# Latent attention on one core: value rows issued in groups of two on every second step, and scores alternated with maxima on the steps between

## The chip, the cores and the metric

The kernel runs on one core of one Trainium2 chip. The metric is the device time of one launch in microseconds, the median of repeated runs. A profile of one further execution shows what each engine did: TensorE (PE in the profile) multiplies matrices, VectorE (DVE) and ScalarE (ACT) work elementwise and read what TensorE leaves in PSUM, GpSimd (POOL) works elementwise in SBUF, and SyncE (SP) issues transfers. The engines have queues of their own and meet at semaphores.

## The reference

The program is a chain of four residual blocks over `x` of shape (4, 1024, 128): causal attention with clipped scores, latent attention with a mixture of experts behind it, a second causal attention, and a low-rank feed-forward block. The change touches the latent attention alone. Its 16 heads share one key per position:

```python
q = (x @ Wq).reshape(b, t, H, D).transpose(0, 2, 1, 3)
ckv = x @ Wkva
kv_latent, k_rope = (ckv[:, :, :R], ckv[:, :, R:])
kv = (kv_latent @ Wkvb).reshape(b, t, H, NOPE).transpose(0, 2, 1, 3)
...
q = jnp.concatenate([q_nope, _rope(q_rope)], axis=-1)
k = jnp.concatenate([kv, _rope(k_rope)], axis=-1)
v = jnp.concatenate([kv, jnp.zeros_like(k_rope)], axis=-1)
att = jnp.einsum('bhqd,bhkd->bhqk', q, k) / jnp.sqrt(jnp.float32(D))
mask = jnp.tril(jnp.ones((t, t), dtype=bool))
att = jnp.where(mask, att, jnp.float32(-jnp.inf))
att = jax.nn.softmax(att, axis=-1)
y = jnp.einsum('bhqk,bhkd->bhqd', att, v)
```

In the kernel `Wkvb` is folded into the queries and into the output weights, so a head works with 16 latent and 32 rotary numbers per position (48 rows), and the softmax's maximum of each query enters the scores as a 49th row.

## The kernel before

Each attention stage runs 16 items (4 sequences times 4 quads of heads); the latent one is called with the name `am`, `latent=True` and `clip=False`. An item is cut by the causal mask into 9 steps, `g` = 0 to 8, and `item` on TensorE (in `attention`) issues for each step, in the order of `ROW_ORDER`, five pieces:

- `score_unit` (L937), twice: keys times queries for two heads, fp32, 49 rows. The two heads use the upper and the lower half of the array's rows. A unit fills two PSUM banks; there are two units of them (`NSB`), so a unit waits for ScalarE's exponential of the unit before the last (`s_e`).
- `max_pair` (L968, with the mask products of L962), twice: queries times keys for two heads in bf16, for an item ahead of the current one by `LEAD` = 4 steps, so that step `g` handles row (g + 4) mod 9 of `MAX_ROWS`. Rows 0, 3, 5 and 7 are one product of 512 columns without a mask, rows 1 and 2 one with a mask, rows 4, 6 and 8 two products. A pair writes two of three PSUM banks (`M_BUFS` = 3). Each bank is read by one `tensor_reduce` on VectorE (L1174), and a pair waits (`s_mr`) until the first reduction of the pair before it is done.
- `value_row` (L989), once: values times probabilities for four heads, fp32, the four heads in four groups of the array's columns. Step `g` handles row `g - PLAG` with `PLAG` = 2, in steps 0 and 1 that is rows 7 and 8 of the item before. A row waits for its exponentials, for GpSimd's masks on the diagonal (`s_sel`, L1127), and rows 0 and 3 also for ScalarE's copy of the output bank (`copy_output`, L1045).

ScalarE takes the score units in order (L1065, an exponential of 128x1024 each) and copies the output bank at steps 2 and 5. Probabilities are kept for six rows (`PRING`), and the exponential of row `g` waits until value row `g - 6` is done. VectorE runs the reductions in order; after row 8 of `MAX_ROWS`, at step 4, `gather_maxima` (L1184, L1186, L1193) puts an item's maxima together before the next reduction. SyncE then carries them through memory into the 49th row of the next item's queries. Before the first item, `first` on TensorE runs 13 rows of `max_pair` with a filler product (L447) behind each pair. The last item has no maxima ahead of it, nor have steps 5 to 8 of the one before; the first item has no values in steps 0 and 1.

Of the kernel before, what the change touches and what calls it, by code (L numbers as in the profile page):

```python
# [36 lines left out]
ROWS_P = (KB * (KB + 1) // 2) * P // UNIT  # L37
# [37 lines left out]
def build(nc, ins, consts, out):  # L75
    stack = ExitStack()
    with stack:
# [601 lines left out]
        def attention(name, scale, latent, clip):  # L679
# [10 lines left out]
            PLAG, PRING = (3 if clip else 2), 6  # L690
# [6 lines left out]
            if clip:  # L697
                ROW_ORDER = (("score", 0), ("score", 1), ("value", 0))
            elif latent:
                ROW_ORDER = (("score", 0), ("score", 1), ("max", 0), ("value", 0), ("max", 1))  # L700
            else:
                ROW_ORDER = (("score", 0), ("score", 1), ("max", 0), ("score", 2), ("max", 1), ("score", 3), ("value", 0))
            DIMS = MD
            KROWS = DIMS + (0 if clip else 1 if latent else 3)
            n_loads = 5 if latent else LOADS8
# [14 lines left out]
            def units(i, g, j, cnt=1):  # L720

                row = (ROWS_P * i + g) % PRING
                if row < RING_ROWS:
                    return ring[:, row * QUAD + j:row * QUAD + j + cnt, :]
                at = (row - RING_ROWS) * QUAD + j
                return pr_buf[:, at:at + cnt, :]
# [41 lines left out]
            def slot(i, off=0):  # L768
                return (i + off) % NB

            def uses(b, i, off=0):

                return b + (i + off) // NB + 1
# [12 lines left out]
            def count_of(eng, b, i):  # L786

                if isinstance(b, int):
                    return b * NQ + i
                count = eng.alloc_register()  # L790
                eng.reg_mov(count, b * NQ + i)
                return eng.snap(count, donate=True, min_val=i, max_val=(BATCH - 2) * NQ + i)

            def max_row(g, last):

                off, r = divmod(g + LEAD, ROWS_P)
                if last is not None and last + 1 + off >= ITEMS:
                    return None
                return 1 + off, r

            with nc.Block() as block:
                @block.sync
                def _(sp):
# [19 lines left out]
                    def maxima(b, i, off):  # L823
# [16 lines left out]
                        for pr in range(2):  # L840
                            if latent:
                                row = ml_d[bass.ds(n, 1), :, :].rearrange("n (a r) t -> n a r t", r=2)[:, :, pr, :]
                            else:
                                row = mx_d[bass.ds(n, 1), :, :, :]\
                                    .rearrange("n c (a r) t -> (n c) a r t", r=2)[:, :, pr, :]
                            sp.dma_start(qs[64 * pr + DIMS:64 * pr + KROWS, s, :, :], row).then_inc(s_mrow[s], 16)

# [78 lines left out]
                def _(pe):  # L926
                    def score_unit(n, i, g, e):
                        t = EXPS_R * g + e
                        bank = s_bank0 + WIDE * (t % NSB)
                        s = slot(i)  # L930

                        wait_alone(pe, s_e, EXPS * n + t + 1)
                        for k, q0, nq, off in S_UNITS[g]:
                            for w in range(WIDE):
                                p, pr = divmod(WIDE * e + w, 2)
                                rows = slice(64 * pr, 64 * pr + KROWS)
                                mm = nc.tensor.matmul(ps[:, bank + w, off * P:(off + nq) * P],  # L937
                                                      keys(rows, s, p, k),
                                                      qs[rows, s, p, q0 * P:(q0 + nq) * P],
                                                      start=True, stop=True)  # L940
                        mm.then_inc(s_s, 1)

                    def max_pair(m, b, i, off, g, p):
# [13 lines left out]
                        for q, k0, nk, o_ in segs:  # L957
# [7 lines left out]
                            for pr in range(2):  # L965
                                rows = slice(64 * pr, 64 * pr + DIMS)
                                kk = slice(k0 * P, (k0 + nk) * P)
# [6 lines left out]
                    def value_row(n, i, g):  # L974

                        s = slot(i)
                        if clip:
                            pe.wait_ge(s_clip, EXPS * n + EXPS_R * (g + 1) + BASE)
                        else:
                            pe.wait_ge(s_e, EXPS * n + EXPS_R * (g + 1) + NSB + BASE)  # L980
                        pe.wait_ge(s_sel, DIAGS * n + diags_before[g + 1] + BASE)
                        half = 0 if g < A_ROWS else 1
                        if g in (0, A_ROWS):
                            pe.wait_ge(s_oc, 2 * n + half + 1 + BASE)
                        for r, k, q0, nq, off in V_ROWS[g]:
                            lo = q0 - 4 * half
                            for j in range(QUAD):
                                v = vs[:, s, k, 0:VW] if latent else vs[:, s, k, j * VS:(j + 1) * VS]
                                mm = nc.tensor.matmul(  # L989
                                    ps[VW * j:VW * j + V_ROWS_OUT, o_bank + half % O_BUFS, lo * P:(lo + nq) * P], v,  # L990
                                    units(i, r, j)[:, 0, off * P:(off + nq) * P],
                                    start=(k == 0), stop=(g in (A_ROWS - 1, ROWS_P - 1)), tile_position=(0, VW * j),
                                    skip_group_check=True)
                        mm.then_inc(s_pv, 1)
# [18 lines left out]
                    def item(b, i, last):  # L1013
                        s = slot(i)
                        n = count_of(pe, b, i)
                        if has_max:
                            pe.wait_ge(s_mrow[s], 16 * 2 * uses(b, i) + BASE)
                        pe.wait_ge(s_ld[s], 16 * n_loads * uses(b, i) + BASE)
                        for g in range(ROWS_P):
                            ahead = max_row(g, last) if has_max else None  # L1020
                            for step, which in ROW_ORDER:
                                if step == "score":
                                    score_unit(n, i, g, which)
                                elif step == "max":
                                    if ahead is not None:
                                        max_pair(n, b, i, *ahead, which)
                                elif g >= PLAG:
                                    value_row(n, i, g - PLAG)
                                elif last != 0:
                                    value_row(n - 1, i - 1, g - PLAG + ROWS_P)  # L1030

                    def rest():
                        for g in range(ROWS_P - PLAG, ROWS_P):
                            value_row(ITEMS - 1, ITEMS - 1, g)

                    run_items(pe, item, first, rest)

                @block.scalar
# [1175 lines left out]
        project_heads8("p0", w_sb["wq0"][:, :], w_sb["wk0"][:, :], w_sb["wv0"][:, :], True)  # L2214
        end_phase()
        attention("a0", 8.0 ** -0.5, latent=False, clip=True)
        end_phase()
        prepare("am")
        finish_and_project_latent(w_sb["wout0"][:, :])
        end_phase()  # L2220
        attention("am", 0.125, latent=True, clip=False)
        end_phase()
        finish_latent()
# [4 lines left out]
        project_heads8("p1", w_sb["wq1"][:, :], w_sb["wk1"][:, :], w_sb["wv1"][:, :], False)  # L2228
        end_phase()
        attention("a1", 8.0 ** -0.5, latent=False, clip=False)  # L2230
        end_phase()
        finish_and_ffn()
# [86 lines left out]
```

## Time and profile before

| | before |
|---|---|
| median of 3 runs | 1818.73 us (1810.61 to 1827.36) |
| the profiled execution: time, span | 1816.31 us, 1814.6 us |
| mean granted clock of TensorE | 0.953 |
| busy over the span: TensorE / VectorE / ScalarE / GpSimd | 88% / 71% / 62% / 37% |
| latent attention: first filler of `first` to the last value matmul | 453.8 to 1005 us |
| its items, from the first score | 508.05 to 1005 us |
| fp32 value rows, fp32 scores, L1174 reductions in all stages | 464.4, 550.0 and 706.7 us busy |

The views used below are the table by stretch (the stretch, its length, then busy us and number of instructions of PE, of PE's weight loads, DVE, ACT and POOL, then TensorE's granted clock, the DMA engines' busy share and GB/s), and the timeline, whose rows are instructions merged by kind: the start in us, the time they took, engine, line, operation, the tiles written and read with their shape, how many, and in brackets how long the engine had been idle before them and which engine's work ended that. The duration of a matmul row holds the modelled time until its results are out, so the difference of two starts tells how long TensorE was occupied. A matmul of fp32 stands in the trace twice.

### The profile page before, as it was taken

What the parts mean: (1) busy time and instruction counts of PE and PEld (TensorE: products, weight loads), DVE (VectorE), ACT (ScalarE), POOL (GpSimd) and SP (SyncE); (2) the same over time, 40 slices, a digit from 0 to 9 for tenths busy, and PEclk for the clock granted to TensorE, in tenths of its full rate; (3) what the DMA queues carried; (4) which work ended last, traced back from release to release, by engine and by line L of the source; (5) the groups of instructions that cost most, each with busy time, mean ns of one, the idle gap of its engine ahead of it and who ended that gap; (6) DMA issues with size and microseconds to landing.
All of it is one profiled execution on the core that took longest, in us unless ns stands there. A gap on an engine that the chain in (4) does not pass through costs nothing. (4 is left out here: it accounts for less than half of the span.)

```text
span 1814.6 us, 36604 instructions
## 1 busy us (share of the span) xinstructions
PE 1598.9 (88%) x12310; PEld 696.2 (38%) x12310; DVE 1293.7 (71%) x2458; ACT 1128.7 (62%) x1788; POOL 674.7 (37%) x1223
## 2 busy tenths in 40 slices
PE   5888888597899999999999888897589999999787
PEld 3422222243344444444444554454333333333233
DVE  6688888676667777777772346664499999999064
ACT  6699999443046565555556434322628888888655
POOL 6566766676313232323222001102513333333373
PEclk9799999799979999999999999988899999999998
DMA  8643434257323131413210400000712222222201
GB/s 236 157 69 58 69 68 135 55 134 174 59 36 78 44 83 43 78 48 72 54 43 25 170 28 1 0 0 1 227 31 52 52 52 52 52 52 70 61 14 47
DMA packets 92080, 125.99 MB, mean 69 GB/s; under 512 B 24533, under 2 KB 64085, under 8 KB 91686
## 3 DMA queue, kind: packets, MB, share of 16 engines
q1 hardware_dynamic: 89814, 121.30, 28.9%
q10 hardware_dynamic: 2096, 2.47, 0.4%
q8 instruction: 101, 1.65, 0.4%
q14 instruction: 69, 0.57, 0.1%
HBM read 76.03 MB, written 47.58 MB: 68 GB/s over the span
## 5 line engine op out<-in xcount | busy, mean ns | idle before, releaser
L1174 DVE TENSOR_REDUCE o_sb<-ps 128x1 f32<-128x512 f32 (+3 forms) x864 | 706.7, 863 | 150.5 <-PE ps L968 143.5
L1065 ACT ACTIVATE q_buf<-ps 128x1024 f32<-128x1024 f32 (+1 forms) x768 | 567.8, 833 | 232.0 <-PE ps L937 230.8
L1127 POOL TENSOR_SCALAR_AFFINE_SELECT q_buf<-q_buf 128x256 f32<-128x256 f32 x432 | 212.9, 515 | 380.9 <-ACT q_buf L1065 320.4
L1065 ACT ACTIVATE pr_buf<-ps 128x1024 f32<-128x1024 f32 (+1 forms) x384 | 286.1, 834 | 63.1 <-PE ps L937 63.0
L989 PE MATMUL ps<-q_buf,v_buf 128*9 128x512 f32 (+7 forms) x2880 | 306.1, 515 | 13.5 <-POOL q_buf L1127 11.7
L937 PE MATMUL ps<-q_buf 48*128 48x512 bf16 (+7 forms) x1536 | 269.6, 330 | 21.6 <-ACT q_buf L1065 5.4
L937 PE MATMUL ps<-q_buf,k_buf 49*128 49x512 f32 (+3 forms) x1536 | 280.4, 492 | 0.0
L1127 POOL TENSOR_SCALAR_AFFINE_SELECT pr_buf<-pr_buf 128x256 f32<-128x256 f32 x336 | 166.3, 520 | 268.6 <-ACT pr_buf L1065 227.3
L937 PEld LDWEIGHTS ps<-q_buf 48*128 48x128 bf16 (+1 forms) x1536 | 78.7, 94 | 255.9 <-ACT q_buf L1065 133.4
L989 PE MATMUL ps<-pr_buf,v_buf 128*9 128x512 f32 (+7 forms) x1728 | 158.3, 459 | 17.5 <-POOL pr_buf L1127 17.5
L937 PEld LDWEIGHTS ps<-q_buf,k_buf 49*128 49x128 f32 x1536 | 143.3, 188 | 71.2 <-issue 46.8
L1234 DVE TENSOR_SCALAR q_buf<-q_buf 128x1024 f32<-128x1024 f32 x192 | 146.2, 770 | 25.0 <-ACT q_buf L1065 22.1
L447 PE MATMUL ps<-w_wg,identity 128*128 128x512 f32 (+1 forms) x214 | 101.7, 598 | 31.0 <-PEq L112 31.0
L968 PE MATMUL ps<-q_buf 48*128 48x512 bf16 (+3 forms) x768 | 119.1, 325 | 7.7 <-DVE o_sb L1174 6.0
L968 PE MATMUL ps<-k_buf,q_buf 48*128 48x512 bf16 (+3 forms) x768 | 121.9, 330 | 4.6 <-DVE o_sb L1174 4.6
L962 PE MATMUL ps<-causal_k,causal_q 64*128 64x128 bf16 x1024 | 107.2, 219 | 15.7 <-DVE o_sb L1174 14.9
L989 PEld LDWEIGHTS ps<-q_buf,v_buf 128*9 128x9 f32 (+1 forms) x2880 | 55.7, 95 | 136.7 <-issue 106.8
L962 PEld LDWEIGHTS ps<-causal_k,causal_q 64*128 64x128 bf16 x1024 | 54.6, 94 | 113.5 <-DVE o_sb L1174 97.2
L1234 DVE TENSOR_SCALAR pr_buf<-pr_buf 128x1024 f32<-128x1024 f32 x96 | 75.0, 788 | 11.5 <-ACT pr_buf L1065 9.8
L316 DVE BATCH_NORM_STATS2 q_buf<-ps 128x6 f32<-128x128 f32 x96 | 21.3, 285 | 80.9 <-PE ps L2055 56.7
L364 ACT ACTIVATE q_buf<-ps,q_buf 128x128 f32<-128x128 f32 x96 | 36.1, 459 | 64.6 <-POOL q_buf L348 64.6
L989 PEld LDWEIGHTS ps<-pr_buf,v_buf 128*9 128x9 f32 (+1 forms) x1728 | 37.0, 96 | 100.5 <-issue 62.5
(184 smaller groups left out, 1750.3 us busy)
## 6 DMA issues: line engine op xcount, KB each, us to landing
q_buf<-qm_d SPq DMA_DIRECT2D x32, 384.0 KB, 6.7
qm_d<-pr_buf SPq DMA_DIRECT2D x80, 128.0 KB, 2.4
o_d<-pr_buf SPq DMA_DIRECT2D x16, 512.0 KB, 2.7
q_buf<-o_d SPq DMA_DIRECT2D x8, 1024.0 KB, 5.0
q_d<-q_buf SPq DMA_DIRECT2D x48, 128.0 KB, 2.1
k_d<-q_buf SPq DMA_DIRECT2D x48, 128.0 KB, 1.9
k_buf<-km_d SPq DMA_DIRECT2D x32, 192.0 KB, 6.8
q_buf<-q_d SPq DMA_DIRECT2D x60, 96.0 KB
```

What stands on the lines that cost most here:

```text
L316: i = nc.vector.bn_stats(self.bn[:, c % 2, t, :], src[:, t, :])
L364: i = nc.scalar.activation(dst[:, t, :], src[:, t, :], ACT.Identity, scale=self.rstd[:, r, t:t + 1], bias=self.minus_m[:, r, t:t + 1])
L447: nc.tensor.matmul(ps[:, bank, 0:columns], identity[:, :], w_sb["wg"][:, 0:columns], start=True, stop=True)
L937: mm = nc.tensor.matmul(ps[:, bank + w, off * P:(off + nq) * P], keys(rows, s, p, k), qs[rows, s, p, q0 * P:(q0 + nq) * P], start=True, st ...
L962: nc.tensor.matmul(ps[:, bank[pr], (o_ + nk - 1) * P:(o_ + nk) * P], causal_q[rows, :], causal_k[rows, :], start=True, stop=False, skip_gr ...
L968: mm = nc.tensor.matmul(ps[:, bank[pr], o_ * P:(o_ + nk) * P], (qm if latent else qs)[rows, s, p, q * P:(q + 1) * P], km[rows, s, kk] if l ...
L989: mm = nc.tensor.matmul(ps[VW * j:VW * j + V_ROWS_OUT, o_bank + half % O_BUFS, lo * P:(lo + nq) * P], v, units(i, r, j)[:, 0, off * P:(off ...
L1065: nc.scalar.activation(units(i, g, WIDE * e, WIDE), ps[:, bank:bank + WIDE, :], ACT.Exp, scale=scale).then_inc(s_e, 1)
L1127: nc.gpsimd.affine_select(out=blk, in_=blk, compare_op=ALU.is_ge, fill=0.0, base=0, pattern=[[0, 2], [1, P]], channel_multiplier=-1)\
L1174: nc.vector.tensor_reduce(to, sc, AX_X, ALU.max).then_inc(s_mr, 1)
L1234: nc.vector.tensor_scalar(two, two, float(np.exp(-10.0)), float(np.exp(10.0)), ALU.max, ALU.min).then_inc(s_clip, 1)
```

## The change

In the latent stage `values_at(g)` now says which value rows a step runs: none in steps 0, 3, 5 and 7; rows 7 and 8 of the item before in step 1; row 0 in step 2; rows 1 and 2 in step 4; 3 and 4 in step 6; 5 and 6 in step 8. So rows 1, 3, 5 and 7 come one step later than before and the others where they were. A step without values issues score, maxima, score, maxima (`NO_VALUE_ORDER`), where a step with values keeps the order of before. No instruction is added or taken away, and the other two attention stages keep their order.

```diff
+            VALUES_AT = {2: (0,), 4: (1, 2), 6: (3, 4), 8: (5, 6), 10: (7, 8)}
+            NO_VALUE_ORDER = (("score", 0), ("max", 0), ("score", 1), ("max", 1))
+
+            def values_at(g):
+
+                if not latent:
+                    return [g - PLAG]
+                return [r for at, rows in VALUES_AT.items() for r in (rows if at == g else
+                                                                      [r - ROWS_P for r in rows] if at == g + ROWS_P else ())]
+
...
                             ahead = max_row(g, last) if has_max else None
-                            for step, which in ROW_ORDER:
+                            rows = values_at(g)
+                            for step, which in ROW_ORDER if rows else NO_VALUE_ORDER:
                                 if step == "score":
                                     score_unit(n, i, g, which)
                                 elif step == "max":
                                     if ahead is not None:
                                         max_pair(n, b, i, *ahead, which)
-                                elif g >= PLAG:
-                                    value_row(n, i, g - PLAG)
-                                elif last != 0:
-                                    value_row(n - 1, i - 1, g - PLAG + ROWS_P)
+                                else:
+                                    for r in rows:
+                                        if r >= 0:
+                                            value_row(n, i, r)
+                                        elif last != 0:
+                                            value_row(n - 1, i - 1, r + ROWS_P)
```

How the steps stand on TensorE: the first piece is of an item in steady state, step 3 and the beginning of step 4, before. L937 are scores, L968 maxima with their masks in L962, L989 values.

```order
L937 MATMUL ps<-q_buf,k_buf 128x512 x4
L968 MATMUL ps<-k_buf,q_buf 128x512 x2
L989 MATMUL ps<-pr_buf,v_buf 32x384 x4
L989 MATMUL ps<-pr_buf,v_buf 32x128 x4
L968 MATMUL ps<-k_buf,q_buf 128x512 x2
L937 MATMUL ps<-q_buf,k_buf 128x512 x4
L962 MATMUL ps<-causal_k,causal_q 128x128 x2
L968 MATMUL ps<-k_buf,q_buf 128x384 x2
L962 MATMUL ps<-causal_k,causal_q 128x128 x2
L968 MATMUL ps<-k_buf,q_buf 128x128 x2
L989 MATMUL ps<-pr_buf,v_buf 32x256 x4
```

The same place of the changed program, where scores are L947, maxima L978 with masks in L972, and values L999.

```order
L947 MATMUL ps<-q_buf,k_buf 128x512 x2
L978 MATMUL ps<-k_buf,q_buf 128x512 x2
L947 MATMUL ps<-q_buf,k_buf 128x512 x2
L978 MATMUL ps<-k_buf,q_buf 128x512 x2
L947 MATMUL ps<-q_buf,k_buf 128x512 x4
L972 MATMUL ps<-causal_k,causal_q 128x128 x2
L978 MATMUL ps<-k_buf,q_buf 128x384 x2
L972 MATMUL ps<-causal_k,causal_q 128x128 x2
L978 MATMUL ps<-k_buf,q_buf 128x128 x2
L999 MATMUL ps<-pr_buf,v_buf 32x384 x4
L999 MATMUL ps<-pr_buf,v_buf 32x128 x4
L999 MATMUL ps<-pr_buf,v_buf 32x256 x4
```

Value row 1 has left step 3 for step 4, and in step 3 one score unit instead of a value row stands between the two pairs of maxima.

The second place is step 5 of the same item on TensorE, behind the pair of maxima after which VectorE gathers. Before:

```order
L937 MATMUL ps<-q_buf,k_buf 128x512 x4
L968 MATMUL ps<-k_buf,q_buf 128x512 x2
L989 MATMUL ps<-q_buf,v_buf 32x512 x4
L989 MATMUL ps<-pr_buf,v_buf 32x256 x4
L968 MATMUL ps<-k_buf,q_buf 128x512 x2
```

The changed program, steps 5 and 6:

```order
L947 MATMUL ps<-q_buf,k_buf 128x512 x2
L978 MATMUL ps<-k_buf,q_buf 128x512 x2
L947 MATMUL ps<-q_buf,k_buf 128x512 x2
L978 MATMUL ps<-k_buf,q_buf 128x512 x2
L947 MATMUL ps<-q_buf,k_buf 128x512 x4
L972 MATMUL ps<-causal_k,causal_q 128x128 x2
L978 MATMUL ps<-k_buf,q_buf 128x512 x2
L999 MATMUL ps<-q_buf,v_buf 32x512 x4
L999 MATMUL ps<-pr_buf,v_buf 32x256 x4
L999 MATMUL ps<-q_buf,v_buf 32x512 x4
```

Value row 3 (512 and 256 columns) has moved behind the first maxima of step 6, where row 4 follows it.

## Rows read from the trace of the kernel before

**Rows 1.** Table by stretch: inside the clipped stage, and latent items in steady state.

```profile
60.00:400.00 340.00, 282.28 (x2459) 82.68 (x2460) 278.38 (x439) 289.80 (x341) 223.95 (x320) 0.95 0.41 84
530.60:999.00 468.40, 463.12 (x4045) 212.14 (x4042) 335.28 (x596) 281.45 (x306) 129.83 (x266) 1.00 0.25 56
```

**Rows 2.** Timeline, TensorE, steps 3 to 5 of one item in steady state.

```profile
742.11 0.40 PE L968 MATMUL ps<-k_buf,q_buf 48*128 48x512 bf16 x2
742.44 1.07 PE L989 MATMUL ps<-pr_buf,v_buf 128*32 128x384 f32 x16
743.45 0.39 PE L968 MATMUL ps<-k_buf,q_buf 48*128 48x512 bf16 x2
743.67 1.90 PE L937 MATMUL ps<-q_buf,k_buf 49*128 49x512 f32 x8
745.39 0.24 PE L962 MATMUL ps<-causal_k,causal_q 64*128 64x128 bf16 x2
...
746.85 0.23 PE L962 MATMUL ps<-causal_k,causal_q 64*128 64x128 bf16 x2 [0.38 <-DVE o_sb L1174]
...
747.19 1.95 PE L937 MATMUL ps<-q_buf,k_buf 49*128 49x512 f32 x8
748.96 0.39 PE L968 MATMUL ps<-k_buf,q_buf 48*128 48x512 bf16 x2
749.29 1.06 PE L989 MATMUL ps<-q_buf,v_buf 128*32 128x512 f32 x8
750.17 0.61 PE L989 MATMUL ps<-pr_buf,v_buf 128*32 128x256 f32 x8
750.72 0.39 PE L968 MATMUL ps<-k_buf,q_buf 48*128 48x512 bf16 x2
```

**Rows 3.** Timeline, VectorE, the same place: reductions and the gathering.

```profile
746.01 1.29 DVE L1174 TENSOR_REDUCE o_sb<-ps 128x4 f32<-128x512 f32 x2 [0.77 <-PE ps L968]
...
748.80 0.22 DVE L1184 TENSOR_REDUCE mx_sb<-o_sb 128x16 f32<-128x64 f32 x1
...
749.49 1.26 DVE L1174 TENSOR_REDUCE o_sb<-ps 128x1 f32<-128x512 f32 x2
```

**Rows 4.** Timeline, TensorE before the first item: pairs with short fillers between.

```profile
477.35 0.39 PE L968 MATMUL ps<-k_buf,q_buf 48*128 48x512 bf16 x2 [0.32 <-DVE o_sb L1174]
...
478.69 0.39 PE L968 MATMUL ps<-k_buf,q_buf 48*128 48x512 bf16 x2 [0.32 <-DVE o_sb L1174]
...
492.67 0.23 PE L962 MATMUL ps<-causal_k,causal_q 64*128 64x128 bf16 x2 [0.32 <-DVE o_sb L1174]
...
494.13 0.39 PE L968 MATMUL ps<-k_buf,q_buf 48*128 48x512 bf16 x2 [0.32 <-DVE o_sb L1174]
...
496.12 0.39 PE L968 MATMUL ps<-k_buf,q_buf 48*128 48x512 bf16 x2 [0.97 <-DVE o_sb L1174]
```

**Rows 5.** Timeline, TensorE: first item, second pair of step 0, and scores of step 1.

```profile
513.42 0.29 PE L962 MATMUL ps<-causal_k,causal_q 64*128 64x128 bf16 x2 [0.95 <-DVE o_sb L1174]
...
514.01 3.64 PE L937 MATMUL ps<-q_buf,k_buf 49*128 49x384 f32 x16
517.43 0.60 PE L968 MATMUL ps<-k_buf,q_buf 48*128 48x512 bf16 x2
```

**Rows 6.** Timeline, ScalarE, output copy and exponentials of step 5, same item.

```profile
748.32 0.60 ACT L1045 ACTIVATE pr_buf<-ps 128x512 f32<-128x512 f32 x1 [1.63 <-PE ps L937]
748.81 1.94 ACT L1065 ACTIVATE q_buf<-ps 128x1024 f32<-128x1024 f32 x2
```

**Rows 7.** Timeline, last item without maxima: one step on TensorE.

```profile
967.92 1.99 PE L937 MATMUL ps<-q_buf,k_buf 49*128 49x512 f32 x8
969.84 1.06 PE L989 MATMUL ps<-pr_buf,v_buf 128*32 128x512 f32 x8
970.84 1.99 PE L937 MATMUL ps<-q_buf,k_buf 49*128 49x512 f32 x8
```

**Rows 8.** Timeline, ScalarE, the exponentials of that step.

```profile
969.10 1.94 ACT L1065 ACTIVATE q_buf<-ps 128x1024 f32<-128x1024 f32 x2 [0.93 <-PE ps L937]
```

## Prediction, made before the changed kernel ran

> **What bounds the kernel now.** The change lies in the latent stage, so I read the table by stretch first. Over 468.4 us of its steady state TensorE is busy 463.1 us at the full clock, VectorE 335.3 and ScalarE 281.5 [rows 1]. TensorE's order of work sets this stage, and whatever it loses or saves per item counts in full. The timeline of one item then shows where TensorE is not computing. Two things are to be seen.
>
> First, the switches between kinds of product. From a pair of maxima to the next scores it takes 0.22 us (743.45 to 743.67), but from the same pair to a value row 0.33 us (742.11 to 742.44), so entering values costs 0.11 us [rows 2]. A 512-column value row followed by another takes 0.88 us (749.29 to 750.17). One followed by maxima takes 1.01 (742.44 to 743.45, 384 and 128 columns), so leaving values costs about 0.13 us. A switch there and back is 0.24 to 0.25 us. Two score units take 1.72 us (743.67 to 745.39), 0.86 each.
>
> Second, one wait in each item, 0.38 us before the second pair of step 4 [rows 2]. The value row between the pairs has only 256 columns. The second pair waits until VectorE has done the first reduction of the first pair. VectorE had been idle for 0.77 us before that reduction [rows 3], so this is not a queue on VectorE: it is the round trip of a bank, 745.39 to 746.85, 1.46 us. The stretch before the first item shows the same trip for the other forms, since TensorE has only short fillers there and always waits: 1.34 us for a pair of one 512-column product (477.35 to 478.69), 1.46 us again for two products (492.67 to 494.13), and 1.99 us where the gathering comes between (494.13 to 496.12) [rows 4]. In steady state the pair after the gathering never waits, because 1.72 us of scores come before it and a value row after it.
>
> The Trainium skill (TensorEngine Tiling (Array Packing), Key Properties) says that changing the tiling mode drains TensorE. The trace agrees: scores and maxima share one mode and cost nothing between them, values use another, with the 0.24 us above. That rule speaks for the change, and taken alone it would give the faster rival below.
>
> **What the change saves.** Per item there were nine value rows, each with its own way in and out. Now there are five groups, so four switches go: 4 x 0.25 = 1.0 us. Step 4 now has rows 1 and 2 between its pairs, which covers the 1.46 us: 0.38 us of waiting goes. Together 1.38 us per item.
>
> **What it costs.** In a valueless step the work between one pair and the next is one score unit. From the last pair of the step before to the first pair there are 0.22 + 0.86 = 1.08 us, and the trip takes 1.34, a wait of 0.26. If the pair has two products, it occupies TensorE for 0.34 us (746.85 to 747.19) [rows 2], and against 1.20 us stand 1.46, again 0.26. A pair with one mask lies between these forms, and its wait the same. So every pair of steps 0, 3 and 7 waits about 0.26 us: 6 x 0.26 = 1.56 us. In step 5 the first pair waits 0.26, but the second waits for a reduction behind the gathering: 1.99 against 1.08, 0.91 us. [rows 3] carry the same sum: from the second pair of step 4 at 746.85 to the next item's first reduction at 749.49 are 2.64 us; with 0.66 for that reduction (half of 1.29 or so) and the 0.15 us by which 746.85 follows the end of the reduction begun at 746.01, the second pair could start 3.45 us on, and 1.46 + 1.99 is 3.45. Waits on VectorE are then 1.56 + 0.26 + 0.91 = 2.73 us per item.
>
> ScalarE adds a little. Two exponentials take 1.94 us, a copy another 0.49 (748.32 to 748.81) [rows 6]. A valueless step of 2.6 us with its waits still holds both, but the score unit that follows sits behind exponentials that started up to 1.1 us after their scores, and at step 5 behind the copy. I take 0.2 us per item, from nothing to 0.5 (the copy's whole length).
>
> Balance of a full item: 2.73 + 0.2 - 1.38 = **+1.55 us**, 5% of it. Items 1 to 13 are full: 13 x 1.55 = 20.2 us.
>
> The others: in item 0 step 0 the two pairs already stood without values between them, with a wait of 0.95 us [rows 5]; a score unit now fills it. The rest of that item has its steps 3, 5 and 7 (2.2 us of waits), and saves three switches and 0.38 us. Sum: about +0.2 us. The last item has no maxima, its step of scores and one value row takes 2.92 us (967.92 to 970.84) and hides ScalarE. Without the values the scores of the next step come after 1.73 us. But the first exponential starts 1.18 us after the scores (969.10 against 967.92), lasts 1.02 and is seen 0.15 later, so its banks are free at 2.35 us: 0.62 us of wait in each of four steps, and the copy's 0.49 once, 3.0 us in all [rows 7, 8]. Switches there cost 0.20 in (969.84 less 967.92 is 1.92, less 1.72) and 0.12 out, so merging four saves 1.3 us: about +1.7. Item 14 is half of one kind and half of the other: +1.3.
>
> Value rows that come one step later cost nothing elsewhere. Their exponentials are older, not younger. Rows of six steps are kept, and no value row is more than three steps behind. The output copies at steps 2 and 5 wait for rows 8 and 2, which are still done in steps 1 and 4. The transfers of maxima begin at the same place of an item.
>
> **Sum.** 20.2 + 0.2 + 1.3 + 1.7 = 23.4 us, and TensorE restarts after about eight waits per item instead of one (scores behind the wait of [rows 2] take 1.77 us, 747.19 to 748.96, against 1.72), of which a few us may show. I take +24. Against the profiled execution's own 1816.3 us this is 1840.3; that execution lies 2.4 us under the median of 1818.7, so I say **1841 us**, 1.2% above that median.
>
> **Rivals.**
> *Faster: the round trip is hidden.* If the pairs of valueless steps did not wait, the 1.38 us of each full item would be all: 13 x 1.38 and a little for the others, 20 us less, 1798 us. It decides at a round trip of 1.08 us instead of 1.34. For it: VectorE is idle 28% of the stage [rows 1]. Against it: the trips of [rows 2, 4] were measured with VectorE idle or just keeping up, and three banks let no pair run further ahead. Break-even would be half the waits. Chance 0.08.
>
> *No change that can be measured: half the waits.* The 1.34 us of [rows 4] may be VectorE's pace of two reductions (1.26 to 1.29 us) and not the trip. A pair that finds VectorE idle could then be quicker, and the first pair of each valueless step would not wait: 4 x 0.26 = 1.04 us less per item, +10 us in all, 1829 us. Against it is the 1.46 us from an idle VectorE. Chance 0.20.
>
> *Slower still: ScalarE binds.* If every score unit of a valueless step waited as in the last item, 0.62 x 4 in place of my 0.2, partly inside the waits on VectorE: +1 us per item, 1855 us. Chance 0.07.
>
> *Slower still: the clock.* At the lower level the scores of one step take 3.42 us (514.01 to 517.43) [rows 5] against 1.72. TensorE will now stand idle about 9% of the stage, in pieces under 1 us. In the clipped stage it is busy 83% of 340 us and the granted clock averages 0.95 [rows 1], so I expect the full clock to hold. If as large a share of the stage were lost as there, 5% of 490 us at the lower level adds some 25 us: 1865 us. The Trainium skill (TensorE: Matmul & The Clock Gate, A second HAM failure mode: psum-queue depth-cycling) describes a kernel whose short idle times between groups made the clock swing between its levels. The latent stage's own waits are too few before the change to test that. Chance 0.06.
>
> *The forecast* keeps 0.59, with 1834 to 1849 for its unknown terms: ScalarE's 0 to 0.5 us per item, switches of 0.24 to 0.32, and restarts.
>
> **Chances.** About 1% is what a measurement of this kernel can tell from no change. Slower by more than that means above 1837: most of the forecast (0.50) and both slower rivals (0.13), 0.63. Within 1%: the rest of the forecast, half the waits, and a part of the faster case, 0.31. Faster: 0.06. The range 1826 to 1856 leaves out the faster case, the clock, and little more.
>
> **What would show it.** In the changed profile: maxima of the valueless steps with an idle time of about 0.26 us released by VectorE, and one of 0.9 us an item, eight such waits instead of one; a spacing of 1.34 us between plain pairs; an item 1.5 us longer than before; TensorE waiting 2.9 us an item where it waited 0.4, and about 1 us an item less spent in switches; two value rows of 512 columns in 1.73 to 1.90 us. The forecast is wrong if those pairs start without idle time, if a score unit between two pairs of maxima takes more than 0.86 us, or if the clock in the stage falls below 1.00.

## The result, and the profile after

| | before | changed |
|---|---|---|
| median of 10 runs each | 1819.16 us | 1833.22 us |
| ratio | | 1.0074, interval 1.0048 to 1.0100 |
| the profiled execution: time, span | 1816.31, 1814.6 us | 1838.42, 1836.7 us |
| mean granted clock in it | 0.953 | 0.950 |
| first to last output copy of the latent stage (ScalarE) | 474.7 us | 495.6 us |
| one latent item in steady state | 31.08 us | 32.34 us |

The change makes the kernel slower, by 14 us in this comparison; one run on each side, of 2225.18 and 1858.23 us, was in the slower state and counts in the medians but not in the ratio. In a second comparison, where the changed kernel ran again, the ratio was 1.0107 (1.0069 to 1.0145), which is 19 us. Both intervals are wide for a difference of this size, and the traces say why: the latent stage behaves the same in each, while the time spent at the lower clock elsewhere does not (below). The item's time here and further on is the distance of the same output copy in two consecutive items.

The stage's length can be read from the output copies, 32 in each kernel. The view is the line's own, with minimum, median and maximum duration in ns and the first and last start in us. Before:

```profile
L1045 ACT ACTIVATE pr_buf<-ps x32: 597/597/598, 530.6 to 1005.3; 128x512 f32<-128x512 f32 x32
```

The changed kernel:

```profile
L1058 ACT ACTIVATE pr_buf<-ps x32: 597/597/597, 527.9 to 1023.5; 128x512 f32<-128x512 f32 x32
```

The first copy comes 2.7 us earlier, the last 18.2 us later. Of the 2.7 us, 0.5 lie before the first item, whose first scores start at 507.56 instead of 508.05. A further part is that TensorE's stretch at the lower clock over the first steps was 17.1 us long in this execution instead of 20.5; it is at most half of the difference, 1.7 us (an estimate). So up to 2.2 us of the 2.7 are luck of this execution. The rest the change had saved by then: the wait of 0.95 us in step 0 that [rows 5] showed and the one of step 4 are gone, less the new waits of step 3.

The timeline of TensorE in the changed kernel, steps 3 to 6 of one item, answers to [rows 2]:

```profile
746.39 0.23 PE L972 MATMUL ps<-causal_k,causal_q 64*128 64x128 bf16 x2
...
746.73 1.04 PE L947 MATMUL ps<-q_buf,k_buf 49*128 49x512 f32 x4
747.85 0.39 PE L978 MATMUL ps<-k_buf,q_buf 48*128 48x512 bf16 x2
748.06 1.04 PE L947 MATMUL ps<-q_buf,k_buf 49*128 49x512 f32 x4
749.18 0.39 PE L978 MATMUL ps<-k_buf,q_buf 48*128 48x512 bf16 x2
749.40 2.04 PE L947 MATMUL ps<-q_buf,k_buf 49*128 49x512 f32 x8
751.24 0.25 PE L972 MATMUL ps<-causal_k,causal_q 64*128 64x128 bf16 x2
...
751.71 1.50 PE L999 MATMUL ps<-pr_buf,v_buf 128*32 128x384 f32 x24
753.14 0.23 PE L972 MATMUL ps<-causal_k,causal_q 64*128 64x128 bf16 x2
...
753.49 1.07 PE L947 MATMUL ps<-q_buf,k_buf 49*128 49x512 f32 x4
754.60 0.39 PE L978 MATMUL ps<-k_buf,q_buf 48*128 48x512 bf16 x2
754.82 1.04 PE L947 MATMUL ps<-q_buf,k_buf 49*128 49x512 f32 x4
756.59 0.39 PE L978 MATMUL ps<-k_buf,q_buf 48*128 48x512 bf16 x2 [0.74 <-DVE o_sb L1187]
```

Read the starts of the maxima, not the brackets. From 746.39 to 747.85 are 1.46 us, to 749.18 another 1.33, from 753.14 to 754.60 again 1.46, and to 756.59, over the gathering, 1.99. These are the spacings of [rows 4] within a hundredth. A score unit between two pairs, 0.86 us of work, now takes 1.12 (748.06 to 749.18). Most of these waits have no bracket, because the modelled end of the matmul before covers them: a row of 1.04 us in a slot of 1.12 looks busy. Over the stage TensorE's busy time hides them in the same way.

Step 8 and step 0 of the next item show the same spacing behind a long group of values, for a pair that finds VectorE waiting for work:

```profile
768.25 0.39 PE L978 MATMUL ps<-k_buf,q_buf 48*128 48x512 bf16 x2
768.48 1.02 PE L947 MATMUL ps<-q_buf,k_buf 49*128 49x512 f32 x4
769.59 0.23 PE L972 MATMUL ps<-causal_k,causal_q 64*128 64x128 bf16 x2
```

and on VectorE:

```profile
768.75 1.29 DVE L1187 TENSOR_REDUCE o_sb<-ps 128x1 f32<-128x512 f32 x2 [0.89 <-PE ps L978]
```

VectorE had been idle for 0.89 us, and the next pair still comes 1.34 us after this one.

VectorE at the second place, with the gathering in between, answers to [rows 3]:

```profile
753.76 1.29 DVE L1187 TENSOR_REDUCE o_sb<-ps 128x4 f32<-128x512 f32 x2 [0.59 <-PE ps L978]
755.09 0.22 DVE L1197 TENSOR_REDUCE mx_sb<-o_sb 128x16 f32<-128x64 f32 x1
755.23 0.39 DVE L1199 TENSOR_REDUCE mx_sb<-o_sb 128x4 f32<-128x16 f32 x4
755.65 0.21 DVE L1206 STREAM_TRANSPOSE mx_turned<-mx_sb 128x32 f32<-128x32 f32 x1
755.78 1.26 DVE L1187 TENSOR_REDUCE o_sb<-ps 128x1 f32<-128x512 f32 x2
```

The maxima written at 754.60 are not read before 755.78, and the second pair starts 0.81 us after that.

### The profile page after: what moved, and what is told of

The parts are those of the page before. It is cut to its first block and busy times, and to the rows that moved or that the text cites. A ratio compares the mean times of both kernels' runs of the same rounds, so it can differ in the third digit from the quotient of the medians.

```text
span 1836.7 us, 36604 instructions
## 1 busy us (share of the span) xinstructions
PE 1605.2 (87%) x12310; PEld 696.0 (38%) x12310; DVE 1293.1 (70%) x2458; ACT 1134.6 (62%) x1788; POOL 675.1 (37%) x1223
## 5 line engine op out<-in xcount | busy, mean ns | idle before, releaser
L999 PE MATMUL ps<-q_buf,v_buf 128*9 128x512 f32 (+7 forms) x2880 | 300.7, 514 | 13.6 <-POOL q_buf L1140 11.6
L947 PE MATMUL ps<-q_buf,k_buf 49*128 49x512 f32 (+3 forms) x1536 | 291.4, 492 | 3.1 <-ACT q_buf L1078 1.9
L947 PE MATMUL ps<-q_buf 48*128 48x512 bf16 (+7 forms) x1536 | 270.1, 331 | 20.4 <-ACT q_buf L1078 5.3
L947 PEld LDWEIGHTS ps<-q_buf 48*128 48x128 bf16 (+1 forms) x1536 | 78.8, 94 | 254.8 <-ACT q_buf L1078 132.9
L999 PE MATMUL ps<-pr_buf,v_buf 128*9 128x512 f32 (+7 forms) x1728 | 154.7, 457 | 17.2 <-POOL pr_buf L1140 17.2
L947 PEld LDWEIGHTS ps<-q_buf,k_buf 49*128 49x128 f32 x1536 | 139.9, 188 | 51.7 <-ACT q_buf L1078 17.7
L978 PE MATMUL ps<-k_buf,q_buf 48*128 48x512 bf16 (+3 forms) x768 | 121.5, 330 | 18.2 <-DVE o_sb L1187 15.3
L978 PE MATMUL ps<-q_buf 48*128 48x512 bf16 (+3 forms) x768 | 119.7, 327 | 7.6 <-DVE o_sb L1187 6.0
L447 PE MATMUL ps<-w_wg,identity 128*128 128x512 f32 (+1 forms) x214 | 96.4, 571 | 30.9 <-PEq L112 30.9
L972 PE MATMUL ps<-causal_k,causal_q 64*128 64x128 bf16 x1024 | 107.3, 220 | 14.1 <-DVE o_sb L1187 8.7
L999 PEld LDWEIGHTS ps<-q_buf,v_buf 128*9 128x9 f32 (+1 forms) x2880 | 59.5, 95 | 132.5 <-issue 97.3
L972 PEld LDWEIGHTS ps<-causal_k,causal_q 64*128 64x128 bf16 x1024 | 53.9, 94 | 126.8 <-DVE o_sb L1187 110.4
L1058 ACT ACTIVATE pr_buf<-ps 128x512 f32<-128x512 f32 x64 | 38.1, 595 | 70.7 <-PE ps L947 66.0
L978 PEld LDWEIGHTS ps<-k_buf,q_buf 48*128 48x128 bf16 x768 | 43.3, 95 | 98.5 <-DVE o_sb L1187 68.6
```

What stands on the lines that cost most here:

```text
L447: nc.tensor.matmul(ps[:, bank, 0:columns], identity[:, :], w_sb["wg"][:, 0:columns], start=True, stop=True)
L972: nc.tensor.matmul(ps[:, bank[pr], (o_ + nk - 1) * P:(o_ + nk) * P], causal_q[rows, :], causal_k[rows, :], start=True, stop=False, skip_gr ...
L978: mm = nc.tensor.matmul(ps[:, bank[pr], o_ * P:(o_ + nk) * P], (qm if latent else qs)[rows, s, p, q * P:(q + 1) * P], km[rows, s, kk] if l ...
L999: mm = nc.tensor.matmul(ps[VW * j:VW * j + V_ROWS_OUT, o_bank + half % O_BUFS, lo * P:(lo + nq) * P], v, units(i, r, j)[:, 0, off * P:(off ...
L1058: nc.scalar.activation(o_two[:, i % 2, half * UNIT:(half + 1) * UNIT], ps[:, o_bank + half % O_BUFS, :], ACT.Copy).then_inc(s_oc, 1)
```

## Experiments

**The changed kernel again.** No edit.

> The changed kernel once more, to see how its time moves with the mean granted clock from run to run and whether its item is always 32.34 us long (before: 31.08). Theory: the stage is 18 to 19 us longer in every run, and what differs between runs lies outside it, in stretches at the lower clock; then the ratio is 1.005 to 1.010 and the item in this trace is 32.3 us again. Rival: the stage itself varies; the item would then differ by more than 0.1 us.

Measured: ratio 1.0107 (1.0069 to 1.0145), and 32.33 to 32.35 us for all but a few items, as in the first trace. The stage is the same to 0.1 us (535.4 to 1031.0, 495.5 us). What moves from run to run is the granted clock outside it, and the runs' times follow it, here for the runs of this comparison and of the changed kernel near the same clock:

| mean granted clock of a run | before, us | changed, us |
|---|---|---|
| 0.948 / 0.949 | 1818.26, 1819.78 (0.949) | 1838.44 (0.948) |
| 0.950 / 0.951 | 1818.31, 1818.72, 1816.24 (0.951) | 1840.94 (0.950) |
| 0.954 | 1815.06, 1815.28, 1815.41 | 1835.92 |
| 0.956 / 0.957 | 1810.65, 1814.21, 1812.02 | 1832.06 |
| 0.961 / 0.962 | 1805.33 (0.961) | 1824.39 (0.962) |

A straight line through the compared runs of this study gives, at a mean clock of 0.955, 1813.0 us for the kernel before (70 runs, 1.2 us less for each 0.001 more of clock, scatter 1.5 us) and 1833.0 us for the changed one (14 runs): **20 us** between them. That fits the trace, where the stage ends 18.2 us later after a start that was up to 2.2 us ahead by luck. The mean is taken over the whole launch, and a longer stage at the full clock raises it a little; at equal time spent at the lower clock the same runs lie 19.4 us apart. The medians of the first comparison differ by less: the changed kernel's compared runs there had a mean clock of 0.956, while the median before, 1819.16 us, lies on its line at about 0.950. (The clocks of those runs of before are not known.) Why the mean clock of one batch is higher than that of another I can't say; that stays open.

**Grouped, but without the alternation.**

```diff
-            NO_VALUE_ORDER = (("score", 0), ("max", 0), ("score", 1), ("max", 1))
+            NO_VALUE_ORDER = (("score", 0), ("score", 1), ("max", 0), ("max", 1))
```

> Value rows grouped as in the changed kernel, but valueless steps keep scores, scores, maxima, maxima. Theory (a pair of maxima waits for the bank's trip over VectorE, 1.34 us): in each of four steps the second pair now stands only 0.22 to 0.34 us behind the first and waits about 1.1 us, 4.5 us per item in place of 2.7; item 34.1 to 34.3 us, about 45 us slower than before (ratio 1.022 to 1.026). Rival (the loss of the change comes from score units that wait for ScalarE, and alternation is what delays them): the item is no longer than 32.3 us and the ratio stays under 1.010.

Measured: 1859.87 us, ratio 1.0257 (1.022 to 1.0294), item 33.92 us. TensorE's timeline of this kernel in two valueless steps, step 5 and step 0:

```profile
701.35 0.38 PE L978 MATMUL ps<-k_buf,q_buf 48*128 48x512 bf16 x2
702.68 0.39 PE L978 MATMUL ps<-k_buf,q_buf 48*128 48x512 bf16 x2 [0.95 <-DVE o_sb L1187]
...
716.82 0.22 PE L972 MATMUL ps<-causal_k,causal_q 64*128 64x128 bf16 x2
...
718.27 0.23 PE L972 MATMUL ps<-causal_k,causal_q 64*128 64x128 bf16 x2 [0.95 <-DVE o_sb L1187]
```

The pairs stand next to each other and still start 1.33 us (701.35 to 702.68) and, with two products, 1.45 us apart (716.82 to 718.27). The spacing does not depend on what TensorE does between them. So the alternation is the better half of the change: without it grouping costs 45 us, with it 20. Score units that wait for ScalarE, which the rival named, are not the cause: in steps 5 and 0 here two of them take 1.77 and 1.72 us, as in the kernel before, and the item grew all the same. The item came out 0.2 us under the expected 34.1 to 34.3, which took the second pair of step 5 to wait for the gathering. In this order both score units come before the first pair, and the gathering is over by then.

**Halved reductions, in the changed kernel and in the one before.** The reductions of the latent stage read 256 of 512 columns, so the maxima leave out half of the keys.

```diff
+                            if latent:
+                                sc = sc[:, :, 0:UNIT // 2] if whole else sc[:, :, :, 0:P // 2]
```

> The changed kernel with reductions in the latent stage over half of each bank (256 of 512 columns), so the maxima leave half of the keys out. A reduction should fall from 0.665 us to about 0.40 and the trip from 1.34 to about 1.07 us, just under the 1.08 us of work between two pairs. Theory: the waits of 2.7 us per item fall to about 0.4 (behind the gathering), the item to 30.0 us, 15 to 18 us under the kernel before (ratio 0.990 to 0.993). Rival (ScalarE): nothing on ScalarE changes, the item stays above 31.5 us.

> The kernel before with the same halved reductions, the maxima leaving out half of the keys. Theory: only the one wait of 0.4 us per item is there to fall, item 30.7 us, ratio 0.996 to 0.998. The difference to the halved changed kernel, 0.7 us per item or more, is then what merging four switches is worth without the waits (less the wait behind the gathering). If the halved changed kernel isn't under this one, grouping saves nothing at all.

Measured: item 31.25 us in the changed kernel (31.17 to 31.33) and 30.55 in the one before; ratios 0.9964 (0.9946 to 0.9982) and 0.991 (0.9875 to 0.9945). The kernel before fell by 0.5 us an item, a little more than expected. Besides that its first copy came 14 us earlier (at 516.5 instead of 530.6 us). About half of this is the stretch before the first item, which [rows 4] show waiting for VectorE all the time: from its first pair of maxima to the first scores it took 29.4 us. The kernel with another order in step 4 has whole reductions and in its second trace no lower clock at that place, and took 36.3 (the kernel before 39.1, in part at the lower clock), so the halved reductions are worth about 7 us there. I had not put that into the ratio I expected; it is also why the halved changed kernel is faster than the kernel before although its item is longer. The rest of the 14 us is the clock: the stretch of 20.5 us at the lower clock over the first steps did not come in this execution. The changed kernel missed its 30.0 us by 1.25. Its waits on VectorE went but for about 0.4 us behind the gathering, as expected, and yet only 1.1 us of time came back. TensorE's timeline of that kernel, a valueless step with the first scores of the next:

```profile
715.02 1.02 PE L947 MATMUL ps<-q_buf,k_buf 49*128 49x512 f32 x4
715.89 0.22 PE L972 MATMUL ps<-causal_k,causal_q 64*128 64x128 bf16 x2
...
716.23 1.02 PE L947 MATMUL ps<-q_buf,k_buf 49*128 49x512 f32 x4
717.09 0.22 PE L972 MATMUL ps<-causal_k,causal_q 64*128 64x128 bf16 x2
...
717.43 2.18 PE L947 MATMUL ps<-q_buf,k_buf 49*128 49x384 f32 x16
719.41 0.41 PE L978 MATMUL ps<-k_buf,q_buf 48*128 48x512 bf16 x2
```

The score units in this valueless step take 0.87 and 0.86 us, so no wait on VectorE is left in it. But the two that follow take 1.98 us (717.43 to 719.41) instead of 1.72. The waits view of the same kernel, over twelve items (who waited for whom, us in total, times, longest), says for whom TensorE's weight loads of scores wait:

```profile
PEld ps L947 <- ACT q_buf L1078: 20.8, 54, 0.9
...
PEld ps L947 <- ACT pr_buf L1078: 6.6, 18, 0.6
```

ScalarE needs 1.94 us for two exponentials [rows 8] and its banks come back after 2.35 us, and a valueless step without waits on VectorE is only 2.16 to 2.4 us long. So a second limit stood right behind the first. The rival was right in this much: ScalarE would have taken most of what a quicker VectorE gives back. It was wrong as to the cause of the loss in the changed kernel as it is, where the same loads waited 9.7 us in as long a stretch, and the spacings of 1.33, 1.46 and 1.99 us are VectorE's.

**Halved exponentials as well.** The exponentials of the latent stage cover 256 of 512 columns per head, so half of the probabilities are stale; the reductions stay halved.

```diff
-                                nc.scalar.activation(units(i, g, WIDE * e, WIDE), ps[:, bank:bank + WIDE, :],
+                                cols = UNIT // 2 if latent else UNIT
+                                nc.scalar.activation(units(i, g, WIDE * e, WIDE)[:, :, 0:cols],
+                                                     ps[:, bank:bank + WIDE, 0:cols],
```

> The changed kernel with halved reductions and also exponentials over half of each bank in the latent stage (256 of 512 columns per head), so half of the keys are missing from maxima and half of the probabilities are stale. Theory now: two limits stand one behind the other in a valueless step, VectorE's trip (1.34 us between two pairs) and ScalarE (two score units in 2.35 us), and with both short the saved switches must show: item 30.55 (the halved kernel before) less 1.15 for the switches, plus 0.3 behind the gathering, 29.6 to 29.8 us. Rival: grouping lengthens the item by something else (restarts of TensorE, the gathering); it then stays at 30.5 us or more.

> The kernel before with both halved, the same parts left out. Theory: ScalarE hides nothing there, so the item stays at 30.5 us as with halved reductions alone, and the doubly halved changed kernel is 10 to 14 us faster than this one. Rival: ScalarE also costs the kernel before something; the item falls by more than 0.2 us.

Measured: item 29.73 us grouped and 30.55 us ungrouped, which is 0.8 us less for grouping, in the bounds given. The kernel before did not gain a hundredth from the quicker ScalarE. Over the stage the copies tell the same, first the grouped kernel:

```profile
L1058 ACT ACTIVATE pr_buf<-ps x32: 597/597/597, 514.6 to 971.2; 128x512 f32<-128x512 f32 x32
```

then the ungrouped one:

```profile
L1045 ACT ACTIVATE pr_buf<-ps x32: 597/597/598, 513.3 to 980.1; 128x512 f32<-128x512 f32 x32
```

456.6 against 466.8 us. The measured ratios, 0.9847 (0.9793 to 0.9901) and 0.9861 (0.9825 to 0.9898), overlap, and by them alone the two could not be told apart; at equal mean clock they lie 11 us apart (4 runs each). Grouping does save its switches. It shows only where both readers of PSUM are fast enough to keep up with a step that has no values in it.

**Where in the item the loss lies.** Three kernels differ from the two given only in `VALUES_AT`. The first leaves step 5 alone without values:

```diff
-            VALUES_AT = {2: (0,), 4: (1, 2), 6: (3, 4), 8: (5, 6), 10: (7, 8)}
+            VALUES_AT = {2: (0,), 3: (1,), 4: (2,), 6: (3, 4), 7: (5,), 8: (6,), 9: (7,), 10: (8,)}
```

> The kernel before with only rows 3 and 4 grouped (step 6), so that step 5 alone is valueless and alternated. Theory: 0.26 us before its first pair, 0.9 before the second because of the gathering, 0.28 saved by one switch: item 31.08 + 0.9 = 31.95 us, 12 to 14 us slower than before (ratio about 1.007). Rival (the loss is spread evenly over the four valueless steps): item 31.4 us.

Measured: 1829.82 us, ratio 1.0075 (1.0046 to 1.0105), item 31.91 to 32.06 us. TensorE's timeline around the gathering:

```profile
723.36 0.23 PE L972 MATMUL ps<-causal_k,causal_q 64*128 64x128 bf16 x2 [0.38 <-DVE o_sb L1187]
...
724.82 0.39 PE L978 MATMUL ps<-k_buf,q_buf 48*128 48x512 bf16 x2
...
726.81 0.39 PE L978 MATMUL ps<-k_buf,q_buf 48*128 48x512 bf16 x2 [0.74 <-DVE o_sb L1187]
```

The old wait of step 4 is kept (0.38) and 1.99 us come again between the two pairs (724.82 to 726.81). The second gives step 5 its value row back in the changed kernel:

```diff
-            VALUES_AT = {2: (0,), 4: (1, 2), 6: (3, 4), 8: (5, 6), 10: (7, 8)}
+            VALUES_AT = {2: (0,), 4: (1, 2), 5: (3,), 6: (4,), 8: (5, 6), 10: (7, 8)}
```

> The changed kernel, but value row 3 stays in step 5 and row 4 alone in step 6, so no valueless step follows the gathering. Theory: 0.9 us less than the changed kernel, item 31.4 to 31.5 us, 5 to 6 us slower than before (ratio about 1.003). Rival as for the run with step 5 alone: item 32.0 us.

Measured: item 31.47 to 31.49 us, as expected. The ratio, 0.9995 (0.9964 to 1.0027), does not show the 5 us; at equal mean clock this kernel lies about 5 us above the one before (8 runs). One valueless step of the four, the one behind the gathering, carries 0.87 of the 1.26 us. The rival of an even spread falls.

The third takes the group that looks best, rows 1 and 2, since it also covers the short row's wait:

```diff
-            VALUES_AT = {2: (0,), 4: (1, 2), 6: (3, 4), 8: (5, 6), 10: (7, 8)}
+            VALUES_AT = {2: (0,), 4: (1, 2), 5: (3,), 6: (4,), 7: (5,), 8: (6,), 9: (7,), 10: (8,)}
```

> The kernel before with only rows 1 and 2 grouped (step 4), step 3 alone valueless. It is the one group that also covers a wait of the kernel before (0.42 us behind the 256-column row). Theory: 0.42 + 0.28 saved, 0.51 for two pairs and about 0.12 for ScalarE lost: item 31.0 us, 0 to 2 us faster than before, within what can be measured. Rival (restarts of TensorE cost more than the rows show): item 31.3 us.

Measured: item 31.00 to 31.08 us, ratio 1.0013 (0.998 to 1.0045). No difference. Even the best of the four groups only pays for itself.

**Another order in one step.** In the kernel before, the short value row gets a score unit beside it:

```diff
+            STEP4_ORDER = (("score", 0), ("max", 0), ("score", 1), ("value", 0), ("max", 1))
...
-                            for step, which in ROW_ORDER:
+                            for step, which in STEP4_ORDER if latent and g == 4 else ROW_ORDER:
```

> The kernel before with step 4 alone in another order: score, maxima, score, value, maxima. The short value row then has a score unit beside it between the two pairs, so the wait of 0.42 us goes, and a wait of 0.26 comes before the first pair. Theory: item 30.9 us, 2 to 3 us faster than before in the stage, hardly to be told in the whole time (ratio 0.997 to 1.000). Rival: the order puts the second score unit later and ScalarE with it, item 31.1 us or more.

> The kernel before with step 4 as score, maxima, score, value, maxima, once more in more rounds. The trace of the first run had an item of 30.90 us against 31.08, which is 2.5 us over the stage (ratio 0.9986), while its times came out at 0.996. Theory: the stage's 2.5 us is all there is, and the ratio lies at 0.997 to 1.000. Rival: something outside the stage gains as well, and the ratio stays at 0.996 or below.

Measured: 1809.67 and 1811.85 us, ratios 0.9959 (0.9927 to 0.9992) and 0.9957 (0.9930 to 0.9984), item 30.90 to 30.96 us. TensorE's timeline of step 4:

```profile
710.56 0.39 PE L969 MATMUL ps<-k_buf,q_buf 48*128 48x512 bf16 x2
710.78 1.04 PE L938 MATMUL ps<-q_buf,k_buf 49*128 49x512 f32 x4
711.90 0.23 PE L963 MATMUL ps<-causal_k,causal_q 64*128 64x128 bf16 x2
...
712.24 1.09 PE L938 MATMUL ps<-q_buf,k_buf 49*128 49x512 f32 x4
713.25 0.64 PE L990 MATMUL ps<-q_buf,v_buf 128*32 128x256 f32 x8
713.83 0.23 PE L963 MATMUL ps<-causal_k,causal_q 64*128 64x128 bf16 x2
```

The second pair follows without a wait; the first one is 1.34 us behind the pair before it (710.56 to 711.90), so 0.26 us of the 0.42 are paid there. This kernel is faster than both given ones. The trace accounts for 2.5 us, and at equal mean clock the two batches lie 2.6 and 2.5 us under the kernel before. The other 5 us or so of the measured ratio go with a higher mean clock in its runs (0.956 against 0.951, and 0.954 against 0.950). By the letter of the second expectation the ratio stayed at 0.996, as the rival said. Nothing in the trace of the stage gains more, and what raises the mean clock was not found: chance, or this order itself, which no run separates.

## Why the prediction was right, and where its sizes were off

**The direction and the mechanism** held. The forecast was +24 us and 1841 us; measured were +14 and +19 us in two comparisons, +18.2 us at the end of the stage in the trace, and +20 us at equal clock. 1833.22 us lies inside the range. Of the classes the less likely one came: the result is within 1% of before, to which I gave 0.31, and not above it, to which I gave 0.63. I had set that bound at 1837 us, and both the sum, 4 us too high, and the clock of the runs moved the result across it.

Two of the signs named for a wrong forecast stand in the profile as it is printed. Seven of the eight pairs start without a bracket, and a score unit between two pairs takes 1.12 us, more than 0.86. They were badly worded: the 1.12 us are the work of 0.86 and the forecast wait of 0.26, of which the modelled end of the matmul covers all but 0.08.

**The round trip of a bank**, taken from the stretch before the first item: 1.34, 1.46 and 1.99 us were expected between pairs, and 1.33 to 1.34, 1.46, 1.39 to 1.40 (with one mask) and 1.99 came. Eight waits an item, 2.7 us in sum, as forecast. That a stretch outside the loop had measured the price of an order that did not yet exist was the best evidence in the profile.

**ScalarE in the last item**: 2.35 us to the next scores were worked out. It is 987.33 to 989.68 here, and 2.83 with the copy (1008.37 to 1011.20):

```profile
987.33 1.99 PE L947 MATMUL ps<-q_buf,k_buf 49*128 49x512 f32 x8
989.68 2.05 PE L947 MATMUL ps<-q_buf,k_buf 49*128 49x384 f32 x16 [0.36 <-ACT q_buf L1078]
...
1008.37 1.99 PE L947 MATMUL ps<-q_buf,k_buf 49*128 49x512 f32 x8
1011.20 2.05 PE L947 MATMUL ps<-q_buf,k_buf 49*128 49x512 f32 x8 [0.84 <-ACT q_buf L1078]
```

The forecast gave the last item 1.7 us. The traces have the stretch from step 5 of item 14 to step 5 of the last item, all without maxima, which grew by 1.84 us (28.13 against 26.29 between the copies).

**The terms that were off** are those of the savings, 1.38 us per item. A switch was sized at 0.24 to 0.25 us: 0.11 in and 0.13 out. The 0.13 compared a row followed by another (0.88) with one followed by maxima (1.01), but the first also pays to start. Rows 7 and 8 in the changed kernel's timeline of TensorE (the row names the first of several widths):

```profile
741.12 1.93 PE L999 MATMUL ps<-q_buf,v_buf 128*32 128x512 f32 x24
742.98 0.39 PE L978 MATMUL ps<-k_buf,q_buf 48*128 48x512 bf16 x2
```

Together they take 1.86 us, against twice 1.01 to 1.02 for two such rows apart, so leaving costs 0.16 to 0.18 and a switch 0.27 to 0.29; four of them 1.1 to 1.16 instead of 1.0. The wait of step 4 was taken from the bracket, 0.38. The value row before the change, ahead of the wait of [rows 2]:

```profile
745.84 0.64 PE L989 MATMUL ps<-pr_buf,v_buf 128*32 128x256 f32 x8
```

To the 746.85 of [rows 2] that is 1.01 us. With the other order in step 4 it is 0.58 us (713.25 to 713.83), so the wait was 0.43. Both together are 0.1 to 0.2 us more.

**ScalarE per full item**, 0.2 us, was right for the changed kernel (1.84 us in step 4 and 1.79 in step 8 for 1.72 us of scores). But the kernel before had 0.12 us of such lengthening of its own (1.77 and 1.79 us in two steps), which I put on one side of the balance only. The item therefore grew by 1.26 and not 1.55 us, and 13 x 0.29 = 3.8 us are the gap between 24 and 20.

**The rivals.** The hidden round trip was ruled out by the spacings. Half the waits, with the first pair of a valueless step free, also: the spacing is 1.34 us behind a VectorE that had been idle for 0.89 (768.25 to 769.59). ScalarE as a further limit was real but stood behind VectorE, where it cost nothing; a rival of its own would have been that both limits lie within 0.2 us of each other. The clock did not fall in the steady state of the stage. Its row in the table by stretch, over the changed kernel's steady state, with the granted clock in the third column from the end:

```profile
530.60:1017.80 487.20, 466.54 (x4038) 209.58 (x4035) 332.55 (x587) 285.26 (x304) 129.83 (x267) 1.00 0.24 54
```

TensorE waited 9% of that stretch in pieces under 1.2 us and kept 2.4 GHz throughout. The Trainium skill's case of short idle times that make the clock swing (TensorE: Matmul & The Clock Gate, A second HAM failure mode: psum-queue depth-cycling) did not occur here, in either version: the granted clock is 1.00 in both. Its rule on the drain at a change of tiling mode (TensorEngine Tiling (Array Packing), Key Properties) agrees with the traces, which give a size for the two modes used here: 0.27 to 0.29 us there and back.

## What to carry to other kernels

A product whose result another engine must read before its bank is free has a minimum spacing, here 1.34 us and more, and the other work of TensorE is what fills it. Before grouping work to save switches, write down each gap between such products and what will be left in it: here a saving of at most 0.29 us opened two gaps that were 0.26 us too short, and in one step of four the second of them was 0.9 us short, because the reader had something else to do. Look for a stretch in which the reader alone sets the pace, such as a prologue; its spacing is the price. What no run here tested is another way out: a fourth bank for the maxima, so that a pair would wait for the pair before the last and not for the last. The output, the scores and the maxima already take all eight (1, 4 and 3).

## What the runs showed of the hardware that was not expected

The mean granted clock accounts for nearly all of the spread between runs: 1.2 us of time for 0.001 of mean clock, leaving a scatter of 1.5 us where the 70 runs of the kernel before reach from 1803.4 to 1831.3. The gain of the order in step 4, 2.5 us (0.14%) by the trace, came out as 2.6 and 2.5 us once runs were compared at the same clock, each with a standard error of 0.6, where the medians said 7.4 both times.

A wait on TensorE may leave no idle time in its rows. Of eight waits per item with 2.7 us in sum only one had a bracket, of 0.74 us for a wait of 0.91, since the modelled end of a matmul reaches up to 0.2 us past the start of what follows without a wait. Distances of starts show all of them.
